# Conv-mixer block with routed experts on one core: 1/sigma of the first norm sent through memory for groups 2 to 4, variances and dt on GpSimd, another order of the steps

## The reference, cut to what matters

```python
x = x + conv_ref(_ln_c(x), ...)          # norm over the 64 channels, eps 1e-6
    zxbcdt = einsum('bhwc,oc->bhwo', x, W_in)          # z 128, xBC 160, dt 8 columns
    dt  = softplus(zxbcdt[..., 288:] + dt_bias)
    xBC = silu(conv3x3_depthwise(xBC) + conv_b)        # x part 128, B 16, C 16
    KV  = einsum('bln,blhd->bhnd', Bm, xs * dA[..., None]);  dA = dt * exp(A_log)
    y   = (einsum('bln,bhnd->blhd', Cm, KV) + xs * D) * silu(z)
    y   = layernorm(y) * ln_g + ln_b;  out = y @ W_out.T
t = tokens(x)
t = t + ffn(_ln_t(t), ...)               # second norm over 64 channels, eps 1e-5
    top 2 of 8 experts by softmax(t @ gate_w + gate_b)
    sum over 8 experts of weight_e * (gelu(t @ W1_e + b1_e) @ W2_e + b2_e)
```

## Time and profile before

| | |
|---|---|
| median of 3 runs | 160.89 us (160.42 to 161.43) |
| the profiled execution | 161.06 us |
| its span | 158.8 us |
| TensorE granted clock, mean over the span | 0.993 |
| busy: TensorE, VectorE, ScalarE, GpSimd | 143.4, 112.3, 93.8, 80.4 us |
| ScalarE table loads in the trace | 12 (1.28 us each) |

### The profile page before, as it was taken

One profiled execution on the slowest core, in us unless ns is written; L12 is line 12 of the kernel. 1 busy time (PEld: TensorE's weight loads), 2 busy tenths in 40 slices (PEclk: granted clock), 3 DMA queues, 4 the chain that ended last, 5 costly groups with the idle time before them and its releaser, 6 DMA issues.

```text
span 158.8 us, 3263 instructions
## 1 busy us (share of the span) xinstructions
PE 143.4 (90%) x1106; PEld 57.3 (36%) x1106; DVE 112.3 (71%) x294; ACT 93.8 (59%) x178; POOL 80.4 (51%) x149
## 2 busy tenths in 40 slices
PE   6889998999999997999999998989879979999950
PEld 1244435563454554343435442224322222222210
DVE  1396977999888885889997889993566952353540
ACT  2265477436883587785689648645547638485430
POOL 7600750484018005647524945535959335779870
PEclk9999999999999999999999999999999999999997
DMA  4910600000000008930001991201990207940022
...
DMA packets 9658, 11.87 MB, mean 75 GB/s; under 512 B 4130, under 2 KB 7594, under 8 KB 9642
## 3 DMA queue, kind: packets, MB, share of 16 engines
...
...
## 4 chain that ended last, share of the span: by engine, by line
PE 64%; DVE 21%; issue 5%; ACT 3%; DMA 3%; SPq 1%; DVEq 0%; ACTq 0%
PE pm L1060 14%; PE pe L1165 8%; PE pe L1180 8%; PE pe L1060 5%; PE pm L1180 5%; PE pm L1165 5%; DVE tmp L939 4%; DMA cw_x<-in_L_conv_conv_w_dram 3%; PE pr L1124 2%; PE pm L1070 2%; PE pr L1110 2%; DVE x L903 2%; PE pm L1078 2%; DVE g L874 1%; DVE xo L898 1%
## 5 line engine op out<-in xcount | busy, mean ns | idle before, releaser
L472 POOL TENSOR_TENSOR acc<-acc,tmp 128x256 f32<-128x256 f32 x54 | 38.3, 733 | 21.7 <-DVE tmp L939 20.9
L636 ACT ACTIVATE hid<-pe,b1T 128x512 f32<-128x512 f32 x48 | 30.2, 681 | 10.5 <-PE pe L1165 10.4
L1165 PE MATMUL pe<-fst,w 64*128 64x512 f32 x96 | 26.5, 627 | 1.4 <-ACT hid L636 1.4
L1180 PE MATMUL pe<-hid,w 128*32 128x512 f32 x192 | 25.5, 601 | 0.9 <-DVE tmp L939 0.6
L939 DVE SCALAR_TENSOR_TENSOR tmp<-pe,b2T,gates 128x512 f32<-128x512 f32 x24 | 17.9, 745 | 10.6 <-PE pe L1180 10.6
L1060 PE MATMUL pm<-pad,wT 64*128 64x512 f32 x108 | 25.1, 600 | 0.0
L663 DVE SCALAR_TENSOR_TENSOR bcc<-bcp,cw_bc,bcc 128x256 f32<-128x256 f32 x32 | 15.5, 483 | 0.9
L636 ACT ACTIVATE hid<-pm,b1T 128x512 f32<-128x512 f32 x16 | 10.1, 684 | 8.7 <-PE pm L1165 6.3
L1060 PEld LDWEIGHTS pm<-pad,wT 64*128 64x128 f32 x108 | 9.9, 185 | 11.9 <-issue 11.9
L417 POOL TENSOR_TENSOR r<-ve,halves 128x8 f32<-128x8 f32 x3 | 5.0, 1676 | 17.7 <-DVE ve L784 17.7
L1165 PEld LDWEIGHTS pe<-fst,w 64*128 64x128 f32 x96 | 7.8, 185 | 15.1 <-issue 15.0
...
## 6 DMA issues: line engine op xcount, KB each, us to landing
gates<-cwd SPq DMA_DIRECT2D x32, 256.0 KB, 5.7
xin<-in_x_dram SPq DMA_DIRECT2D x6, 128.0 KB, 3.4
out_dram<-acc SPq DMA_DIRECT2D x6, 128.0 KB, 2.5
w<-in_L_ffn_W_dram SPq DMA_DIRECT2D x2, 256.0 KB, 4.9
xin<-in_x_dram ACTq DMA_DIRECT2D x2, 128.0 KB, 4.2
w<-in_L_ffn_W_dram ACTq DMA_DIRECT2D x1, 256.0 KB, 4.4
...
```

Of the source, the lines that this page charges most:

```text
L472: ins = pool.tensor_tensor(acc[p][:, half], (x2 if e == 0 else acc)[p][:, half], tmp[ln][e % 2][:, half], ALU.add)
L636: act.activation(hid[ln][e % 2][:, q, :], expert_banks(g)[q][:], ACT.Gelu, bias=b1T[:, e:e + 1]).then_inc(hid_in[ln].sem, 1)
L1165: ins = pe.matmul(expert_banks(g)[q][:], w1[half, place(e, q), :], fst[p][half, :], start=True, stop=True)
L1180: ins = pe.matmul(bank[C * q + c:C * q + c + BC, half], w2[:, e, c:c + BC], hid[ln][e % 2][:, q, half], start=True, stop=True)
```

## The change

* The taps' load cw_x is issued second and has its own semaphore. W_in's halves have one each, and `twc` becomes `twx` (for the convolution, early) and `twz` (for z, later). Taps 0 to 3 are made on ACT (`tpa`), 4 to 8 on DVE.
* SP issues both halves of x of group 1, ahead of its half of W1; ACT's issue of one half goes.
* `rb` and `rx` are left only for group 0 (`rb`). For groups 1 to 3: POOL's pow writes r1 (now 128 x 32, zeros behind the eight columns), DVE turns it (`rn`), SP writes 16 KB to memory, waits, and reads it back broadcast over the channels in two reads (`rs`); `xn` reads that tile from SBUF.
* The variance operations of all norms but group 0's first go from DVE to POOL, ahead of the pow. dt's scaling, bias and absolute value (`dt1`, `dtv`, three operations) become `dtp` on POOL, four operations; `dtT` on DVE is the transpose of group 0.
* W1's two halves are counted apart, so `bd0` waits for one of them only.
* PLAN is a new list. bT, the experts' rings and the stores are as before; from u31 on the order within each engine is nearly the same.

The diff, cut to its core:

```diff
             load(0, (0,))
-            sp.dma_start(wxz_raw[:, 1], twice(W_in[0:DI, :])).then_inc(d_proj, 16)
-            sp.dma_start(cw_x[:], cw_v[0:DI, :]).then_inc(d_proj, 16)
+            sp.dma_start(cw_x[:], cw_v[0:DI, :]).then_inc(d_cwx, 16)
+            sp.dma_start(wbd_raw[:], twice(W_in[2 * DI:2 * DI + BC + NH, :])).then_inc(d_wbd, 16)
+            sp.dma_start(wxz_raw[:, 1], twice(W_in[0:DI, :])).then_inc(d_z, 16)
+            load(1)
             sp.dma_start(w1[0:C, :, :], W1.rearrange("e c f -> c e f")).then_inc(d_w1, 16)
-            sp.dma_start(wbd_raw[:], twice(W_in[2 * DI:2 * DI + BC + NH, :])).then_inc(d_wbd, 16)
-            load(1, (0,))
...
+                if step == "rs":
+                    sp.wait_ge(rowed.sem, rowed.at(g - 1, 1))
+                    sp.dma_start(rows_d[g].rearrange("r (k t) -> k r t", k=TJ),
+                                 r1t[p][:]).then_inc(d_turned[g], 16)
+                    sp.wait_ge(d_turned[g], 16)
...
+                    rows_g = rows_d[g][0:NT].rearrange("(j q) t -> q j t", q=2)
+                    for q in range(2):
+                        sp.dma_start(r1w[p][C * q:C * q + C, :].rearrange("c (j t) -> c j t", j=TJ),
+                                     rows_g[q].unsqueeze(0).broadcast_to([C, TJ, P])).then_inc(d_row[g], 16)
...
+        def variance(engine, c, at, stats, squares, var, out, eps):
+            mean, mean_sq = stats
+            engine.tensor_tensor(squares[:], mean, mean, ALU.mult).then_inc(c.sem, 1)
+            engine.wait_ge(c.sem, at + 1)
+            engine.tensor_tensor(var[:], mean_sq, squares[:], ALU.subtract).then_inc(c.sem, 1)
+            engine.wait_ge(c.sem, at + 2)
+            engine.tensor_scalar(out, var[:].rearrange("p j q -> p (j q)"), 0.0, eps, ALU.max, ALU.add).then_inc(c.sem, 1)
...
                 if step == "pw":
...
+                    pool.wait_ge(turned.sem, turned.at(g, 1))
+                    variance(pool, var_eps, var_eps.at(g, 0), (t1[p][:, 0, :, 0:2], t1[p][:, 1, :, 0:2]), mq[p], vv[p],
+                             ve[p][:], 1e-6)
...
+                elif step == "dtp":
...
+                    pool.wait_ge(rstd.sem, rstd.at(g, 1))
+                    pool.tensor_tensor(dtv[p][:].rearrange("p (j q) h -> p j q h", q=2),
+                                       t1[p][:, 0, :, 2:2 + 2 * NH].rearrange("p j (q h) -> p j q h", h=NH),
+                                       r1[p][:, 0:NT].rearrange("p (j q) -> p j q", q=2).unsqueeze(3)
+                                       .broadcast_to([P, TJ, 2, NH]), ALU.mult).then_inc(c.sem, 1)
...
+                    pool.tensor_tensor(dtv[p][:], dtv[p][:], dtb[:].unsqueeze(1).broadcast_to([P, NT, NH]),
+                                       ALU.add).then_inc(c.sem, 1)
...
+                    pool.tensor_scalar(dtm[p][:], dtv[p][:], 0.0, 2.0, ALU.max, ALU.mult).then_inc(c.sem, 1)
...
+                    pool.tensor_tensor(dta[p][:], dtm[p][:], dtv[p][:], ALU.subtract).then_inc(c.sem, 1)
...
+                elif step == "tpa":
+                    act.wait_ge(i_tap, 2)
+                    act.wait_ge(d_cwx, 16)
+                    for t in range(4):
+                        act.activation(taps[:, t, :], wxz[:, 0].rearrange("p r c -> p (r c)"), ACT.Copy,
+                                       scale=cw_x[:, t:t + 1]).then_inc(i_tpa, 1)
...
-                elif step == "rx":
...
+                elif step == "rn":
+                    if g > 2:
+                        dve.wait_ge(d_turned[g - 2], 16)
+                    dve.wait_ge(rstd.sem, rstd.at(g, 1))
+                    dve.transpose(r1t[p][:], r1[p][:]).then_inc(rowed.sem, 1)
                 elif step == "xn":
...
-                    dve.wait_ge(spread.sem, spread.at(g, 1))
+                    if g == 0:
+                        dve.wait_ge(spread.sem, spread.at(0, 1))
+                    else:
+                        dve.wait_ge(d_row[g], 32)
                     dve.tensor_tensor(interior(pad[p]), xin[g][:].rearrange("p (b h w) -> p b h w", b=2, h=HH),
-                                      b1[:].rearrange("p (b h w) -> p b h w", b=2, h=HH), ALU.mult).then_inc(normed.sem, 1)
+                                      (r1w[p] if g else b1)[:].rearrange("p (b h w) -> p b h w", b=2, h=HH),
+                                      ALU.mult).then_inc(normed.sem, 1)
```

255 lines of the change are left out of this document (125 added, 130 removed).

## The result

The changed kernel takes 161.47 us (median of 20 runs, 161.14 to 162.34), the one before 160.79 (20 runs, 160.06 to 161.43): ratio 1.0056, 95% interval 1.0042 to 1.0070. It is 0.7 us slower, where 2.3 us less were forecast. It lies inside the outer range, on the other side of no change. Its profiled execution took 162.34 us with a span of 160.5 (before: 161.06 and 158.8); 13 of its runs lie near 161.3 and 7 near 162.1, the profiled one among the upper. The first experiment ran the same kernel again with a profile of the lower bunch (161.67, span 159.9), which is used for sums.

The account below looks back on a forecast made before the run. TensorE bounds 28.7 to 92 us; then VectorE's and ScalarE's answers set the pace. Start -1.05, rb -1.0, middle +0.2, rn2 +0.6, relief -0.5, bubble -0.6: -2.35, so 158.6 us; own range 157.8 to 159.9, outer 156.7 to 161.9.

Parts of the forecast that it names:

- gates +0.5: First group's experts: d10 arrives 0.5 us before its gates, taking 0.5 from the 1.1 us gained at 61 us.
- rn2 in front of y10: Ahead of pj0: y10 queues behind rn2's wait for GpSimd's pow; 0.6 us lost, between 0.2 and 1.2.
- VectorE's relief: 92 to 128 us: 1.8 us of VectorE work gone, half (0.9) counted; net gain 0.5 after 0.4 for longer chains.
- my last item: Closing item: fewer ScalarE table switches, moved c0 and the order from group 1's second expert on change nothing.
- Start: Up to cv20's end: W1 lands and wa begins at 8.6, cv20 ends at 20.15 against 21.21; gain 1.05 us.
- rb of groups 1 to 3: TensorE: dropped transposes, 0.51 us each time, win nothing in group 1 and 1.0 us in groups 2 and 3.
- group 1's middle: Between y0 and cv01: bd1 adds its 0.43 there, sm2 comes some 0.2 earlier; net 0.2 us lost.
- Row through memory: xn of groups 1 to 3: the row's trip through memory costs 0 us, bounded 0 to +1.6.
- Variances and dt on GpSimd: Norms and dt: VectorE gives up 9 to 10 us; gain 0.5 us, bounds -1.9 and +3.3.
- that rule: Skill's shared SBUF port rule: moving work between VectorE and GpSimd might not help; relief of 0.9 nothing, sum 159.5.
- The rival that had GpSimd's chains set the pace: 92 to 128 us: three GpSimd chains (gst3, ve22, ve23), 1.1 us more each, +3.3, giving 162.4; chance 0.15.
- Gap at 61 us: Before sm3: the 1.15 us wait for kvc2 goes; 1.1 less 0.5 for gates, gain 0.6 us.

Follow-up runs that it names:

- e0: The changed kernel run again unchanged, beside the kernel before: 161.47 us, ratio 1.0048.
- e3: The changed kernel with the kernel before's order from m23, group 3's third weighing, on: 162.0 us, ratio 1.0079.
- e15: e11 with the variances on VectorE: 161.47 us, ratio 1.0015.
- e16: e15 with SP's half of W1 issued ahead of group 1's x: 160.58 us, ratio 0.9979.
- e11: The kernel before's order without the row through memory, with the changed kernel's start and small steps on GpSimd: 162.72 us, ratio 1.0151.
- e13: e5 with rb1, xn1, bd1 and bcp1 back where they stood in the kernel before: 161.9 us, ratio 1.0058.
- e1: The changed kernel with only rn2 moved behind y10 in VectorE's order: 160.44 us, ratio 0.9981.
- e7: e1 with all variances back on VectorE: 160.61 us, ratio 0.9992.
- e5: The changed kernel in its new order without the row through memory, TensorE's rb for groups 1 to 3 restored: 162.83 us, ratio 1.0120.
- e4: The changed kernel's code in the kernel before's order, translated step by step, rn2 behind y10: 177.36 us, ratio 1.0982.
- e17: e16 with s22 and ve22 (group 2's second norm) moved behind y3 and u01: 162.61 us, ratio 1.0117.
- e12: e1 with group 2's second norm moved earlier between cwt1 and cwt2: 166.55 us, ratio 1.0325.
- e14: e12 with SP's half of W1 issued ahead of group 1's x: 166.49 us, ratio 1.0322.
- e6: e1 with ps3 moved behind d31: 161.87 us, ratio 1.0062.
- e9: e1 with SP's half of W1 issued ahead of group 1's x: 160.26 us, ratio 0.9983.

## Why the prediction was wrong

The forecast's terms, sorted into the stretches above, against the repeat run of the changed kernel less before:

| stretch | forecast, us | measured, us |
|---|---|---|
| start to y0 | -1.25 | -0.17 |
| y0 to cv02 | +0.5 | +1.24 |
| cv02 to cwt0 | 0 | -0.26 |
| cwt0 to sm3 | -1.1 | -0.35 |
| sm3 to cwt1 | 0 (gates +0.5, rb3 -0.5) | +0.32 |
| cwt1 to cwt3 | -0.5 | +0.84 |
| cwt3 to the last addition | 0 | +0.04 |
| last addition to the end | 0 | -0.56 |
| sum | -2.35 | +1.10 (spans 159.9 and 158.8) |

Some of the experiments differ from each other in one thing only and form a chain from the kernel before to the changed one. Its links, from y0 to cwt3, by the marks of one profiled execution each (profiles of one order and code, as e0, e3 and the first one, or e15 and e16, agree there within 0.1 us):

| link, in us | y0 to sm3 | sm3 to cwt1 | cwt1 to cwt3 | sum |
|---|---|---|---|---|
| dt's first half to GpSimd (before to e16) | +0.01 | -0.32 | -0.04 | -0.35 |
| variances to GpSimd, old order (e16 to e11) | -0.33 | +0.51 | +1.16 | +1.34 |
| new order (e11 to e13) | +0.33 | +0.68 | -0.25 | +0.76 |
| row through memory, rb gone (e13 to e1) | -0.41 | -0.55 | -0.02 | -0.98 |
| rn2 in front of y10 (e1 to e0) | +1.03 | 0 | -0.01 | +1.02 |

The size of a link depends on where it stands. With the variances last (e7 to e1) they gain 0.23 instead of costing 1.34, and the new order with the row through memory (e16 to e7) then costs 1.35 instead of gaining 0.22.

**The step that failed** is the sum from 61 us on. I had hidden the longer norm chains "where TensorE is full", had counted half of VectorE's relief as a gain (0.5 net), and had given the rest of the new order no term at all: my last item covers "the order from the second expert of group 1 on (nearly the same)", while the moves of pj2, rbg2 and s22 stand ahead of that. From sm3 to cwt3 I expected -0.5 us and got +1.16. There the variances on GpSimd cost 1.65 us in the old order (e11 against e15) and 0.48 in the new one (e1 against e7), and the new order costs 0.43 with them on GpSimd (e13 against e11) and, with the row through memory, 1.05 with them on VectorE (e7 against e16). My reading of it: a full TensorE hid a longer chain only as long as products of other work stood ahead of what the chain feeds. In the new list pj2 is taken early and rbg2 late: the timeline of VectorE before has gst2's transpose and s22's at

```profile
85.81 0.32 DVE L885 STREAM_TRANSPOSE tg<-pr 128x128 f32<-128x128 f32 x1 [0.92 <-PE pr L1124]
...
93.78 0.45 DVE L911 STREAM_TRANSPOSE t<-pr 128x256 f32<-128x256 f32 x1 [0.65 <-PE pr L1137]
```

and after at

```profile
87.74 0.31 DVE L941 STREAM_TRANSPOSE tg<-pr 128x128 f32<-128x128 f32 x1
...
96.97 0.45 DVE L960 STREAM_TRANSPOSE t<-pr 128x256 f32<-128x256 f32 x1 [0.28 <-PE pr L1184]
```

that is 3.4 and 11.3 us after cwt1 before, 4.9 and 14.1 after. From the second transpose VectorE walks the router's list to cw, which cwt2 needs; cwt2 now waits 0.83 us for it, where it waited 0.27 for fst. The transpose is 2.8 us later after cwt1 and cwt2 only 0.9: before, this chain had slack. No variant of the code moved this stretch in the new order (24.99, 25.06 and 24.99 in e1, e7 and e5), while in the old one it is 24.1 with the variances on VectorE (e16), 24.3 in e4 and 24.7 in e11. So the order alone makes it 25.0; the variances on GpSimd alone make it 24.7 in the old order, and the two don't add up. That the late norm is the link in it is the reading of these rows, supported by e17, and not shown: e12 and e14 were spoilt.

**Start (forecast 1.05).** The path behind wa was right (to the end of cv20 11.6 us, forecast 11.55), the time at which wa could begin wrong. In seven profiles with this start (the first one, e0 to e3, e6, e7) it begins between 8.92 and 9.57 us instead of at 8.6, and y0 starts 0.63 us earlier to 0.02 later than before; 0.17 in the repeat. Two things held wa, and they end close together. In five of the seven W1's load came last, as in the repeat:

```profile
9.38 0.64 PE L1026 MATMUL pr<-w,centring 64*64 64x512 f32 x1 [0.30 <-DMA w<-in_L_ffn_W_dram]
```

I had let it land at 8.6. In the other two TensorE's own queue came last, for which I had no term: the first four transposes of the taps start at 6.89, the statistics and four warm-up products come behind them, and these end at 9.06. The view puts the 0.45 us ahead of those transposes down to a constant from GpSimd. The kernel's code has them wait for ScalarE's scaling of the taps and for a GpSimd step that had long been done, and ScalarE's timeline fits:

```profile
5.47 1.28 ACT L571 ACTIVATE taps<-wxz,cw_x 128x128 f32<-128x128 f32 x4 [0.51 <-DMA cw_x<-in_L_conv_conv_w_dram]
```

It ends at 6.75, 0.14 us before the transposes start (in e9 6.56 and 6.70). So the change's own move of four taps to ScalarE is part of what holds wa. e9 shows both ends: with W1 earlier wa starts at 8.80, right behind the warm-ups.

**rb of groups 1 to 3 (forecast 1.0, less 0.2 in group 1's middle).** Right: e13 against e1 has 1.2 us by the ratio and 1.0 by the marks. The reading that bd1 left a gap and would cost its length was right too.

**rn2 in front of y10 (forecast +0.6).** The mechanism was right, the size 1.0 us by e0 against e1, inside its bounds. Mis-sized was the time to the pow's end: from its first variance operation 3.4 us, where 2.8 were forecast. The pow took 2.19 us instead of 1.68; it started 0.03 us behind VectorE's g times sz, which reads two tensors from SBUF. The first variance operation took 0.47 beside xn1. Both fit the waiting that I had priced for xn alone.

**Row through memory (0).** Right. No xn waited for its row in the new order; in the old one TensorE waited 5.9 and 4.1 us for two of the rows (e4).

**Variances and dt on GpSimd (forecast -0.5).** Wrong in size, and for the variances in sign where the order wasn't made for them. In the new order 0 to 0.2 us (e7 against e1, within their intervals); in the old one they cost 1.65 us of the marks from 61 us on and 1.3 in all. dt's first half gained 0.35 us of the marks (e16). The small operations took 0.20 to 0.26 us as forecast, in nine chains of eleven. What was wrong is that VectorE's relief would be worth half of itself: it was 6.2 us and not 9 to 10, and from 92 us on, where I had counted it, it shortened nothing. The Trainium skill, "Perfetto Trace Analysis", Optimizing Scalar/DVE Operations, warns that such a move "might not help"; by that rule the sum had been 159.5. The variances' runs agree with it (e7 against e1), dt's link, with 0.35 us gained, does not. The rival that had GpSimd's chains set the pace (0.15) is what e11 shows in the old order, at half of its price (1.65 of 3.3) and by another way: six chains at 0.27 us each, spread over 61 to 130 us, and not three at 1.1. One reading behind that rival was wrong too. I took the 226 ns of the earlier trace rows as the router's line with GpSimd quiet, but that operation starts at 121.53, and two accumulations take 120.68 to 122.34 on GpSimd.

**Gap at 61 us (forecast -0.6, after 0.5 for gates).** The gap went, but the stretch gained 0.35 to 0.43, not 1.1: xt12's four transposes had moved into it, from the stretch ahead, which is 0.26 shorter. m00's wait for its gates is 1.7 us (1.8 before, over 2 expected) and TensorE has none ahead of d10, so the 0.5 for gates was not there either; net near the forecast.

**The end.** The last addition on VectorE starts 1.66 us later than before in the repeat, but the span is only 1.1 longer. Its last stores, before and in the repeat (timeline, issues):

```profile
154.86 1.75 SPq L299 DMA_DIRECT2D out_dram<-acc  x2
154.86 1.75 ACTq L299 DMA_DIRECT2D out_dram<-acc  x2
```

```profile
156.52 1.13 SPq L307 DMA_DIRECT2D out_dram<-acc  x2
156.53 1.40 ACTq L307 DMA_DIRECT2D out_dram<-acc  x2
```

From issue to the end of the span it is 3.94 and 3.38 us, and 4.32 in the profiled execution of the changed kernel with issues of 2.12. The changed kernel's two bunches of times lie nearly as far apart as that. Whatever gains under 0.9 us on TensorE's marks can be taken back or doubled there in a single execution. What decides it is open; e3 moved group 2's store and had 3.6.
